# Attention's image weights turned on TensorE, with a new order of ScalarE's work and a new share-out of the scaling

## The reference

```
h = fq_act(einsum('bnc,mc->bnm', fq_act(x_s), fq_weight(w_s)) + qkv_b)   # 12 heads of 16
attn = fq_act(einsum('bhnd,bhmd->bhnm', q, k) * 16 ** -0.5)
exp_int = floor(polynomial(r) * 2.0 ** (30 - qf))     # integer exponential, by octaves
rounds  = round_ln(round(sum(exp_int) / exp_int))     # power of two nearest to 1 / share
attn = where(rounds >= 16, 0, 2.0 ** -clip(rounds, 0, 15))
out = fq_act(einsum('bhnm,bhmd->bhnd', attn, v)) -> projection -> fq_act
```

## Time and profile before

| | |
|---|---|
| time, median of 3 runs | 1036.82 us (1031.38 to 1037.0) |
| the profiled execution's own time | 1037.42 us |
| its span, first to last instruction | 1035.6 us |
| mean granted TensorE clock, share of full | 0.837 |
| busy in the whole span | DVE 881.2 us (85%), ACT 711.9 (69%), PE 707.6 (68%), POOL 170.0 (16%) |
| DMA | 54.71 MB, 53 GB/s on the mean |

### The profile page before, as it was taken

How to read it: one execution, slowest core, us unless ns; L and a number is a source line. 1 busy time by engine, 2 the same in 40 slices (tenths; PEclk the granted TensorE clock), 3 DMA queues, 4 the chain that set the end, 5 groups by cost and what they waited for, 6 DMA issues and landing times. The chain is left out here.

```text
span 1035.6 us, 22661 instructions
## 1 busy us (share of the span) xinstructions
PE 707.6 (68%) x5955; PEld 482.3 (47%) x5956; DVE 881.2 (85%) x2422; ACT 711.9 (69%) x1376; POOL 170.0 (16%) x274
## 2 busy tenths in 40 slices
PE   3783386747888366676667666676635385999997
PEld 3562244425555233443334333343323244989996
DVE  6888997888888799999999999999978864666766
ACT  0335465957888699898988889999945294555553
POOL 5851410016664000000000000000004530000000
PEclk9985598988999687778887887877756597999999
DMA  8000000001111111111111111111022004355452
GB/s 256 3 2 0 0 1 1 0 1 39 37 37 37 36 28 24 27 25 23 25 24 24 24 24 24 24 23 24 12 89 78 18 1 152 135 186 204 165 197 83
DMA packets 84271, 54.71 MB, mean 53 GB/s; under 512 B 53704, under 2 KB 83176, under 8 KB 83976
## 3 DMA queue, kind: packets, MB, share of 16 engines
q1 hardware_dynamic: 83208, 54.11, 17.2%
q0 software_dynamic: 1024, 0.13, 0.3%
HBM read 11.90 MB, written 3.76 MB: 15 GB/s over the span
## 5 line engine op out<-in xcount | busy, mean ns | idle before, releaser
L1357 DVE SCALAR_TENSOR_TENSOR expo<-expo,con,pow 128x153 f32<-128x153 f32 x480 | 146.1, 374 | 0.8 <-ACT expo L1266 0.8
L1140 PE MATMUL at_rem<-word,ident_half 128*128 128x459 f16 x160 | 66.4, 415 | 102.7 <-ACT expo L1266 101.5
L1266 ACT ACTIVATE expo<-at_rem,con 128x459 f32<-128x459 f32 x160 | 95.4, 640 | 14.5 <-PE at_rem L1141 13.7
L952 DVE TENSOR_REDUCE rs_ends<-rs_banks 128x770 f32 (+1 forms) x96 | 89.2, 957 | 13.5 <-PE rs_banks L924 11.4
L873 ACT ACTIVATE rs_banks<-rs_banks 128x770 f32<-128x770 f32 x96 | 74.6, 796 | 23.2 <-PE rs_banks L916 22.1
L1222 ACT ACTIVATE word<-at_banks 128x459 uint8<-128x459 f32 x160 | 81.0, 560 | 10.4 <-PE at_banks L779 10.2
L1400 DVE CUSTOM_DVE_ANT_0 weight_top<-weight_top,line 128x2448 uint16<-128x2448 uint16 x64 | 86.1, 1345 | 2.1 <-ACT line L1258 2.1
L1140 PEld LDWEIGHTS at_rem<-word,ident_half 128*128 128x128 f16 x160 | 15.7, 98 | 152.8 <-ACT expo L1266 148.1
L1258 ACT ACTIVATE line<-weight_top 128x1224 f32<-128x1224 f32 x64 | 74.0, 1158 | 15.0 <-DVE weight_top L1385 14.7
L774 PE MATMUL at_banks<-pick,row_top 128*128 128x459 bf16 x160 | 73.1, 457 | 11.0 <-ACT word L1222 4.0
L1906 ACT ACTIVATE qk<-e_p,b1s 128x153 f32<-128x153 f32 x192 | 58.9, 392 | 29.3 <-PE e_p L1867 28.1
(11 more groups left out here) (390 smaller groups left out, 2085.2 us busy)
## 6 DMA issues: line engine op xcount, KB each, us to landing
qk<-vt SPq DMA_DIRECT2D x64, 384.0 KB, 3.1
rs_kb<-qk SPq DMA_DIRECT2D x128, 28.7 KB, 1.9
kb<-qk SPq DMA_DIRECT2D x128, 28.7 KB, 1.9
patches<-in_patches SPq DMA_DIRECT2D x4, 768.0 KB
vi<-vt SPq DMA_DIRECT2D x32, 96.0 KB, 2.0
out<-vi SPq DMA_DIRECT2D x32, 96.0 KB, 1.8
pj_w<-in_w SPq DMA_DIRECT2D x1, 2304.0 KB, 8.2
qb<-qk SPq DMA_DIRECT2D x128, 6.0 KB, 1.8
```

Source lines behind the costliest of these rows:

```text
L952: v.tensor_reduce(ends[:, :, n, 5 * b:5 * b + 5], banks[:, slot(u, b), :, 0:5 * W].rearrange("p i (t n) -> p i t n", n=W), AX, ALU.max).th ...
L1140: pe.matmul(out, identh[:, :], bank(word, b).bitcast(F16), start=True, stop=False)
L1266: act.activation(bank(ex, b), rem[:, (u + b) % 2, 0:3 * N], ACT.Square, scale=2.0 ** 24, bias=c(5)).then_inc(sq_done, 1)
L1357: ins = v.scalar_tensor_tensor(ex[:, t, :], ex[:, t, :], c(7), pw[:, t, :].bitcast(BF16), ALU.add, ALU.mult, accum_out=tot[:, t:t + 1])
```

## The change

- `pi`, `pk` and VectorE's transpose are gone, with `corner` on ScalarE and three of the semaphores. In the last turn, TensorE transposes the 32 last columns of each text tile straight from `high`, as 12 transposes of 128 x 32 which land in four groups of 32 partitions, and the corner of the image tiles by 12 small matmuls with 32 x 32 blocks of the identity, into the free end of the same PSUM bank.
- ScalarE's ranks of the last turn get a third instruction, for that corner.
- `pT_all` now holds the image's turned weights as 3 x 153 columns in one piece (`imT`), so that `weighted` makes 3 image products in place of 6.
- VectorE scales 11 tiles, ScalarE 4. Both wait for the last turn of the batch before, as that reads `top`.
- ScalarE writes line 0 and line 1, and then makes all five squares.
- At the start, GpSimd clears `row_top` and `zero`, where VectorE did, and ScalarE makes its first copy before it waits for the constants.

```
-    HALF = 8
+    HALF, OWN = 8, H - 1
...
-        pi, pk = sb("p_image", [P, H, 32], BF16), sb("p_both", [P, HT, 32], BF16)
-        pall = sb("pT_all", [P, H * N + HT * (P + 32)], BF16)
+        pall = sb("pT_all", [P, RT * N], BF16)
...
+        imT = pall[:, H * N:RT * N].rearrange("p (t n) -> p t n", n=N)
...
+        def corner_at(slot):
+            return pT[:, slot, 6 * P:6 * P + 2 * HT * 32].bitcast(F32)
+        def corner_high(slot):
+            return pT[:, slot, 6 * P:6 * P + 2 * HT * 32].rearrange("p (t n two) -> p t n two", t=HT, two=2)[:, :, :, 1]
...
 gpsimd
+                pool.memset(row_top[:, :, :], 0.0).then_inc(words_set, 1)
+                pool.memset(zero[:, :], 0.0).then_inc(words_set, 1)
                 pool.memset(word[:, :, :], WORD).then_inc(words_set, 1)
...
 tensor, turn
-                        if g == GROUPS - 1:
-                            pe.wait_ge(pi_done, n + 1)
...
-                            src = high[:, t, 0:NT] if t < RT else pi[:, 4 * (t - RT):4 * (t - RT) + 4, :].rearrange("p j n -> p (j n)")
-                            mm = pe.transpose(pT[:, slot, j * P:(j + 1) * P], src, identb[:, :])
+                            if t < RT:
+                                mm = pe.transpose(pT[:, slot, j * P:(j + 1) * P], high[:, t, 0:NT], identb[:, :])
+                            else:
+                                for q in range(4):
+                                    mm = pe.transpose(pT[32 * q:32 * q + 32, slot, j * P:(j + 1) * P], high[:, 4 * (t - RT) + q, IW:N], identb[:, :])
+                        if g == GROUPS - 1:
+                            for t in range(HT):
+                                for j in range(4):
+                                    r = slice(32 * j, 32 * j + 32)
+                                    mm = pe.matmul(corner_at(slot)[r, 32 * t:32 * t + 32], high[:, H + t, IW:N], identb[:, r], start=True, stop=True, skip_group_check=True)
                         mm.then_inc(tr_done, 1)
...
 tensor, weighted
-                        pe.matmul(po[p:p + 64, q:q + NT], lhs, piT[:, t, :], start=False, stop=False, skip_group_check=True)
-                        pe.matmul(po[p:p + 64, q + NT:q + N], lhs, pjT[:, t, ID:32], start=False, stop=False, skip_group_check=True)
+                        pe.matmul(po[p:p + 64, q:q + N], lhs, imT[:, t, :], start=False, stop=False, skip_group_check=True)
...
 scalar
-                def corner(n):
-                    if not first(n, 1):
-                        act.wait_ge(tr_done, n * GROUPS)
-                        act.wait_ge(pk_done, n)
-                    act.wait_ge(i_done, n * 2 + 2)
-                    act.activation(pi[:, :, :].bitcast(I16), high[:, 0:H, IW:N].bitcast(I16), ACT.Copy).then_inc(pi_done, 1)
-                    rank(pk[:, :, :], high[:, H:RT, IW:N]).then_inc(pj_index, 1)
...
-                            rank(piT[:, :, :], slot[:, 3 * P:6 * P].rearrange("p (t n) -> p t n", n=P)).then_inc(ev_done, 1)
+                            rank(imT[:, :, 0:NT], slot[:, 3 * P:6 * P].rearrange("p (t n) -> p t n", n=P))
+                            rank(imT[:, :, NT:N], corner_high((u + g) % 2)[:, :, ID:32]).then_inc(ev_done, 1)
...
 scalar, both_shares
-                        act.wait_ge(pj_index, n)
-                    for t in range(H, RT):
+                        act.wait_ge(tr_done, n * GROUPS)
+                    for t in range(OWN, RT):
...
 scalar, body
-                        corner(last[0])
                         ranks(last[0], last[1])
                     if mid is not None:
                         both_shares(mid[0])
-                    for h, which in enumerate(((0, 1), (2, 3, 4))):
-                        if mid is not None:
+                    if mid is not None:
+                        for h in range(2):
                             line_of(mid[0], h)
-                        if now is not None:
-                            squares(now[0], now[1], which)
+                    if now is not None:
+                        squares(now[0], now[1], (0, 1))
+                        squares(now[0], now[1], (2, 3, 4))
-                act.wait_ge(words_set, 1)
-                act.wait_ge(set_up, 4)
...
+                act.wait_ge(words_set, 1)
                 keep_tops(0)
+                act.wait_ge(words_set, 3)
+                act.wait_ge(set_up, 3)
...
 vector
-                v.memset(row_top[:, :, :], 0.0).then_inc(set_up, 1)
-                v.memset(zero[:, :], 0.0).then_inc(set_up, 1)
+                v.sem_inc(set_up, 1)
...
-                            v.wait_ge(pj_index, nb)
+                            v.wait_ge(tr_done, nb * GROUPS)
                         for h, half in enumerate(halves):
-                            if not first(nb, 1):
-                                v.wait_ge(tr_done, nb * GROUPS - 1 + h)
-                            heads = slice(half.start, min(half.stop, H))
+                            heads = slice(half.start, min(half.stop, OWN))
...
-                        v.wait_ge(pj_index, nj + 1)
-                        if not first(nj, 1):
-                            v.wait_ge(pv_done, nj)
-                        v.transpose(pjT.rearrange("p t n -> p (t n)"), pk[:, :, :].rearrange("p t n -> p (t n)")).then_inc(pk_done, 1)
                         v.wait_ge(ev_done, nj * GROUPS + GROUPS)
-                        v.wait_ge(pk_done, nj + 1)
```

More of the change, by code:

```diff
@@ L1018, in attention @@
         vbs, zero = sb("v_image_row", [P, 2, HT * 4 * HD], BF16), sb("zero_column", [P, 2], BF16)
-        pi, pk = sb("p_image", [P, H, 32], BF16), sb("p_both", [P, HT, 32], BF16)
-        pall = sb("pT_all", [P, H * N + HT * (P + 32)], BF16)
+        pall = sb("pT_all", [P, RT * N], BF16)
         ptT = pall[:, 0:H * N].rearrange("p (h n) -> p h n", n=N)
-        piT = pall[:, H * N:H * N + HT * P].rearrange("p (t n) -> p t n", n=P)
-        pjT = pall[:, H * N + HT * P:H * N + HT * (P + 32)].rearrange("p (t n) -> p t n", n=32)
+        imT = pall[:, H * N:RT * N].rearrange("p (t n) -> p t n", n=N)
         high = top[:, :, :].bitcast(BF16).rearrange("p w (n two) -> p w n two", two=2)[:, :, :, 1]
@@ L1033, in attention @@
         ends_done = k.sem("at_ends_done")
-        pi_done, pj_index, pk_done, pj_done, tr_done, ev_done, pv_done, out_done = sem(
-            "pi_done", "pj_index", "pk_done", "pj_done", "tr_done", "ev_done", "pv_done", "out_done")
+        pj_done, tr_done, ev_done, pv_done, out_done = sem(
+            "pj_done", "tr_done", "ev_done", "pv_done", "out_done")
         pj_loaded, a_done = k.sem("pj_loaded"), k.sem("at_a_done")
@@ L1132, in remainder @@
                 def remainder(n, u, which):
+                    if first(n, 1):
+                        pe.wait_ge(set_up, 3)
                     pe.wait_ge(evicted, n * NB + NB)
@@ L1166, in weighted @@
                             pe.wait_ge(out_done, half)
+                        else:
+                            pe.wait_ge(words_set, 2)
                         pe.matmul(po[:, 0:1], identb[:, :], zero[:, 0:1], start=True, stop=False, skip_group_check=True)
@@ L1202, in _ @@
                 turn_tops(0)
-                pe.wait_ge(set_up, 4)
                 scores(0, 0, 0, range(0, 3))
```

## The result

The changed kernel takes 1033.11 us (median of 8 runs) against 1036.61: ratio 0.9965, 95% interval 0.9953 to 0.9977. It is 0.35% faster, where 1.1% slower was forecast; less than the 1% that was called telling, but clear of zero. Its profiled execution took 1034.92 us (span 1033.1), 1.8 above its median.

The account below looks back on a forecast made before the run. VectorE was taken to bound the kernel at 12.54 us a batch, then ScalarE at 13.00. +13.3 us over 29 batches less 2.1 at the start gave +11.2, a median of 1048; own range 1045 to 1060, for all 1022 to 1060.

Parts of the forecast that it names:

- What bounds the kernel: Attention's batches: VectorE full at 12.54 us each, ScalarE's chain 12.05; after the change ScalarE bounds at 13.00.
- VectorE's saving: VectorE per batch: transpose, one share tile and a shorter subtract save 0.55 us, 12.54 to 11.99; floor 12.16 with line wait.
- The squares: ScalarE's five squares in a row wait for TensorE's products 1.05 us a batch, against 0.58 before: +0.47.
- The last turn: TensorE's transposes, tiles and corners ahead of ScalarE's third rank write: +0.5 us a batch, bounds +0.2 to +1.3.
- W: Added time of TensorE's last turn per batch; +0.62 if starts of matmuls never lie closer than about 25 ns.
- The second change inside the turn: TensorE's last turn: a change of tile shape between the 128x32 tiles and the 32x32 corners, 0.10 us.
- The third write of the last turn: ScalarE's added rank instruction for the image corner, 75 elements: 0.17 us a batch.
- the fourth share tile: ScalarE scales one more tile per batch: 0.31 us, at most 0.35.
- The words: ScalarE's part ahead of the ranks: length taken as unchanged, plus 0.1 us of wait for TensorE's first turn.
- The sum: ScalarE's chain per batch: 12.05 - 0.02 + 0.5 + 0.47 = 13.00 us, +0.46 a batch, +13.3 us over 29 batches.
- The start: Start of attention: ScalarE's earlier first copy brings the first octave, and so the total, forward by 2.1 us.
- rival B: A draw: half of the forecast's waits, ScalarE's chain at 12.4 to 12.9 us, 1031 to 1045, middle 1038; chance 0.30.

## Why the prediction was wrong

- **What bounds the kernel:** right in the main. VectorE had 12.54 us, and ScalarE's chain of 12.05 was the one to watch. It did become the bound, but mainly in the batches at half clock; the forecast had it on the whole. So VectorE's busy share fell to 96% and not to 92%.
- **VectorE's saving:** right; 11.99 us was forecast, and 12.00 is what it takes where nothing holds it up. Its floor with the wait for line 0 is 12.32, not 12.16. The ready time of line 0 was given 0.05 us for the signal, which no row shows; the add starts 2.86 us after the shares, not 2.73. In the forecast the share tile's 0.17 us and the 0.17 of wait for line 0 cancel, so the tile was worth nothing to that floor from the start; I overlooked this, and expected 12.49 for the run with three tiles.
- **The squares:** right. +0.47 was forecast, +0.52 came. The first wait of 0.6 us and the last of 0.3 at half clock stand in the timeline.
- **"The last turn ... I take +0.5 us": this step failed.** (It is the "W" of one sentence there.) The terms at full clock gave 0.34, and I moved up to 0.5 for a turn that slides into the half clock. It seldom did: the granted clock over the first two rank writes rose from 0.91 to 0.97 (mean of the same 25 batches), and from the start of the second rank write to that of the third it took 0.27 us longer on the mean (0.74 to 1.01). In 22 of the 25 the turn ran at full clock and cost 0.23 (0.78 us from its first transpose to the third rank write, 0.55 before); two at half clock make up the rest. Of the terms, the tiles (0.17 against 0.18) and the first change of shape (0.10) were right. The second change inside the turn does not exist, as the corners have the tiles' shape, and the three rounds of corners start within 0.06 us, where 0.15 was given. The third write of the last turn took 0.11, not 0.17, the fourth share tile 0.31 as said.
- **The words failed too:** "ranks can begin only when the first turn is there ... I take 0.1", with the words at their old length. They got 0.10 shorter. The clock from the first word to the fifth rose from 0.57 to 0.65. In the kernel before, this part takes 2.81 us at half clock and 2.17 at full (batches without the output copy), so that rise is worth 0.10 us by estimate; with the idle matmuls the part falls to 2.57. I had looked at the clock where it would cost and not where it would give.
- **The sum:** the ranks came out 0.32 and the words 0.20 us a batch below the forecast, squares and shares 0.07 above: 0.45, or 13 us in 29 batches, the whole of the +13.3 that did not come. The run with more corners tests the larger half of this: with ranks of 2.78 us, nearly the forecast's 2.83, the kernel is slower than before (1.0053), but at 12.82 us a batch and not 13.02; most of what still lacks is the words, 2.86 there and not 3.04.
- **The start:** the octave came 2.2 us earlier within attention (2.1 forecast), but the first line only 0.8: the second batch's words met scores at half clock, and the second octave waited 0.93 us for them. Not forecast at all: 1.2 us at the end, where the corner lay open.
- The time is that of rival B, at 0.30, and in part by luck: B wanted the turn at +0.3 (0.27 came) and the squares at +0.3 (0.52 came). The forecast's own range, 1045 to 1060, missed the time, and its sign was wrong; only the wide range over all cases held it.

That VectorE's saving is lost in the batches at half clock is shown by the batches' lengths and the idle matmuls. That the clock falls less over the words is read from the profile; why it does is not shown.

## What to carry to other kernels

A change that takes work from the full engine is worth the room of the second one: here 0.49 us of wait stood against 0.55 saved, and every term put on the second engine counted against that. Before a reorder is priced, follow the path through both engines: a tile in the second half of a step that another engine overlaps is not on it. Nor should two kinds of batch be judged by their mean, as each has its own bound. And where an engine's clock follows its own load, work that is idle can be worth 0.6% behind a change and nothing ahead of it.

## What the runs showed of the hardware

Twelve idle matmuls a batch took the granted clock of TensorE from 0.82 to 0.96, and the kernel went 6 us faster. Ahead of the third product TensorE stands idle for 2.1 to 2.9 us in the kernel before and for 3.2 to 3.7 in the changed one:

```profile
559.72 0.37 PE L1149 MATMUL at_rem<-word,ident_half 128*128 128x459 f16 x1 [3.41 <-ACT expo L1275]
572.05 0.56 PE L1149 MATMUL at_rem<-word,ident_half 128*128 128x459 f16 x1 [3.63 <-ACT expo L1275]
```

In the changed kernel the clock falls to 1.2 GHz once a batch, in 8 of 24 batches in that gap and in 16 in the products behind it. With the idle matmuls the gap is at most 1.6 us and the clock falls 7 times in the same 301 us.

Small matmuls in different column groups of the array start almost together. The 12 corners (128 rows, 32 columns, 32 streamed columns) come in rounds of four, one to each group of 32 columns. Within a round the starts lie at most 6 ns apart; a group's next one starts 25 to 29 ns later at the full clock. The 24 more of the run with more corners cost 0.20 us there, 8 ns each. The Trainium skill (TensorE: Matmul & The Clock Gate, "Wait — 56ns, not 53.3ns?") puts the least distance of two starts near 25 ns. From one matmul to the next the trace does not agree; within one column group it does.
